# Value products of both heads in one product with a block-diagonal stationary operand

## The reference

```python
def _mhsa(x, Wq, Wk, Wv, Wr):
    B, n, D = x.shape
    dh = D // HEADS
    q = (x @ Wq).reshape(B, n, HEADS, dh)
    k = (x @ Wk).reshape(B, n, HEADS, dh)
    v = (x @ Wv).reshape(B, n, HEADS, dh)
    scores = jnp.einsum('bihd,bjhd->bhij', q, k)
    attn = jax.nn.softmax(scores, axis=-1)
    out = jnp.einsum('bhij,bjhd->bihd', attn, v).reshape(B, n, D)
    out = out + x @ Wr
    return jax.nn.relu(out)
...
embed_x = emb_table[X + offsets[None, :]]
att = embed_x
for i in range(LAYERS):
    att = _mhsa(att, WQ[i], WK[i], WV[i], WR[i])
att_output = jax.nn.relu(att.reshape(B, FLAT) @ Wlin)
h = embed_x.reshape(B, FLAT)
h = jax.nn.relu(h @ W1 + b1)
h = jax.nn.relu(h @ W2 + b2)
dnn_output = jax.nn.relu(h @ W3 + b3)
return jax.nn.sigmoid(att_output + dnn_output)
```

## Time and profile before

| What | Value |
|---|---|
| median of 3 runs | 2033.41 us (2029.62 to 2035.76) |
| profiled execution, its span | 2034.7 us |
| TensorE matmuls / weight loads busy | 94% / 83% of the span |
| VectorE / ScalarE / GpSimd busy | 83% / 66% / 44% |
| value products (L496), matmuls | 24576 |
| scores (L479), matmuls | 12288 |
| transposes (L464) | 3072 |

### The profile page before, as it was taken

The page is one execution under the profiler, slowest core; times in us unless marked ns, Lnnn a source line. Parts: engine busy times, 40 slices in busy tenths (PEclk is TensorE's granted clock), DMA queues, the critical chain, the costliest instruction groups (busy, mean ns, idle before and its releaser), DMA issues.

```text
span 2034.7 us, 105018 instructions
## 1 busy us (share of the span) xinstructions
PE 1914.9 (94%) x44960; PEld 1692.9 (83%) x44960; DVE 1690.5 (83%) x3771; ACT 1351.5 (66%) x3609; POOL 893.3 (44%) x949
## 2 busy tenths in 40 slices
PE   1499999999999999999999999999999999999998
PEld 0387888888888888888888888888888888888887
DVE  3477889889898888979888898888889898888987
ACT  1366666667666676766766776666776667676665
POOL 6544354444535454354544435354453545444000
PEclk9899999999999999999999999999999999999998
DMA  4210111111111111111111111111111111110000
GB/s 113 60 31 25 31 27 32 29 30 31 28 33 28 31 30 29 32 28 32 29 30 30 29 33 27 32 28 30 31 28 34 28 32 29 30 31 26 20 20 16
DMA packets 67859, 64.71 MB, mean 32 GB/s; under 512 B 24056, under 2 KB 54792, under 8 KB 67400
## 3 DMA queue, kind: packets, MB, share of 16 engines
q1 hardware_dynamic: 47432, 37.52, 6.3%
q0 software_dynamic: 19968, 20.49, 5.3%
HBM read 27.24 MB, written 0.01 MB: 13 GB/s over the span
## 4 chain that ended last, share of the span: by engine, by line
PE 86%; DVE 5%; issue 4%; ACT 3%; another core or an unknown queue 1%; POOL 1%; SPq 0%; DMA 0%; ACTq 0%
PE SV L479 20%; PE Ob L496 14%; PE X L464 12%; PE X L457 8%; PE X L459 5%; PE X L458 5%; PE Mb L432 3%; PE Mb L433 3%; PE Mb L434 3%; PE Ob L457 3%; PE Ob L458 2%; PE Ob L459 2%; PE Ob L423 2%; PE Mb L450 1%
## 5 line engine op out<-in xcount | busy, mean ns | idle before, releaser
L355 POOL DMA_INDIRECT emb<-L_rec_emb_table,idx_t x624 | 646.9, 1037 | 752.4 <-PE Ob L496 551.2
L742 DVE TENSOR_REDUCE den<-sd 103x16 f32<-103x624 f32 x384 | 308.0, 802 | 225.6 <-ACT sd L616 211.0
L479 PE MATMUL SV<-yv,xs 64*39 64x142 f32 x12288 | 456.0, 285 | 21.2 <-ACT v_sb L618 13.4
L479 PEld LDWEIGHTS SV<-yv,xs 64*39 64x39 f32 x12288 | 349.8, 113 | 68.0 <-issue 39.6
L600 ACT ACTIVATE xs<-Ob 128x312 f32<-128x312 f32 x256 | 110.4, 431 | 383.6 <-PE Ob L496 383.6
L722 DVE TENSOR_REDUCE mx<-SV 103x8 f32<-103x312 f32 x768 | 332.7, 473 | 37.0 <-PE SV L479 28.7
L496 PEld LDWEIGHTS Ob<-pt,v_sb 39*32 39x32 f32 x12288 | 272.1, 106 | 96.5 <-issue 96.0
L464 PE MATMUL X<-ident,pn 103*103 103x103 f32 x3072 | 343.0, 255 | 0.0
L496 PE MATMUL Ob<-pt,v_sb 39*32 39x39 f32 x12288 | 326.4, 198 | 8.9 <-issue 8.5
L332 POOL COPY xs<-embT 64x256 f32<-64x256 f32 x300 | 239.1, 797 | 211.6 <-ACT embT L560 80.7
L727 DVE TENSOR_TENSOR sd<-SV,mx 103x312 f32<-103x312 f32 x768 | 330.2, 470 | 0.1
(11 more groups left out here) (81 smaller groups left out, 2749.2 us busy)
## 6 DMA issues: line engine op xcount, KB each, us to landing
v_x<-v_sb SPq DMA_DIRECT2D x768, 39.0 KB
emb<-L_rec_emb_table,idx_t POOLq DMA_INDIRECT x624
xs<-L_rec_W SPq DMA_DIRECT2D x19, 256.0 KB
w<-L_rec_W SPq DMA_DIRECT2D x1, 512.0 KB
idx_in<-r_X SPq DMA_DIRECT2D x1, 312.0 KB, 3.8
b_b<-L_rec_b SPq DMA_DIRECT2D x1, 256.0 KB
b_b<-L_rec_b SPq DMA_DIRECT2D x1, 128.0 KB
w_b<-L_rec_W SPq DMA_DIRECT2D x1, 128.0 KB
```

The source lines that it names most:

```text
L355: nc.gpsimd.indirect_dma_start(out=emb[:, n % ER, f % 2 * D:(f % 2 + 1) * D], out_offset=None, in_=table, in_offset=bass.IndirectOffsetOnA ...
L479: last = nc.tensor.matmul(SV[64 * b:64 * b + F, at:at + YR], x_pair(u, e, p), yv[64 * e:64 * e + D, l, p, :], start=True, stop=True, skip_ ...
L742: nc.vector.tensor_reduce(den[:], pe_sb[:], AX.X, ALU.add).then_inc(den_ready, 1)
```

## The change

The 64-column padding of the probabilities goes: `pn` has 39 columns a head, so a transpose takes 78 columns and `pt` has 78 partitions, head 0 on 0 to 38 and head 1 on 39 to 77. The values of both heads go into one stationary operand `v_bd` of 78 rows and 64 columns: head 0's values in rows 0 to 38 and columns 0 to 31, head 1's in rows 39 to 77 and columns 32 to 63, zeros elsewhere, written once at the start. One product a sample gives both heads. All values reach `v_bd` by transfers, four a unit; `v_sb` and `v_bd` are laid out with the region innermost, so that each transfer writes 1024 bytes side by side in a partition, and the columns of a stationary operand stand eight elements apart. The copy to `v_sb` reads SV in that order. `VS` becomes 2; SyncE waits for the products of two units before, and ScalarE for the transfers of two units before.

```diff
--- before.py
+++ after.py
@@ -43,7 +43,7 @@
     G = UP
     SR = 256
     YR = HF + D
-    VS = 3
+    VS = 2
     PS = 2
     XS = 5
 
@@ -144,15 +144,15 @@
         x_lo = sb("x_lo", [128, XS, C], F32R)
         w_all = embT[:, 1].rearrange("q c b -> q (c b)")[:, 0:L * (3 * 128 + D)].rearrange("q (l c) -> q l c", l=L)
         yv = sb("yv", [128, L, UP, YR])
-        v_sb = sb("v_sb", [KR, VS, H, G, DH])
-        v_x = sb("v_x", [KR, VS, G, DH])
+        v_sb = sb("v_sb", [KR, VS, H, DH, G])
+        v_bd = sb("v_bd", [HF, VS, 2, D, G])
         mx = sb("mx", [KR, G, H])
         sd = sb("sd", [KR, G, H, F])
         pe_sb = sd
         den = sb("den", [KR, G, H])
         rd = sb("rd", [KR, G, H])
-        pn = sb("pn", [KR, PS, G, H, 64])
-        pt = sb("pt", [KR, G, 2, F])
+        pn = sb("pn", [KR, PS, G, H, F])
+        pt = sb("pt", [HF, G, 2, F])
         red = sb("red", [128, TILES * NP])
         w_in = red[0:D, 0:2 * L * D].rearrange("q (k d) -> q k d", d=D)
         wT = red[0:D, 2 * L * D:4 * L * D].rearrange("q (k d) -> q k d", d=D)
@@ -172,7 +172,7 @@
 
         sv_regions = SV[0:KR, :].rearrange("q (g w) -> q g w", w=SR)
         sv_scores = sv_regions[:, :, 0:HF].rearrange("q g (h f) -> q g h f", f=F)
-        sv_values = sv_regions[:, :, HF:HF + D].rearrange("q g (h c) -> q h g c", c=DH)
+        sv_values = sv_regions[:, :, HF:HF + D].rearrange("q g (h c) -> q h c g", c=DH)
 
         ld_w = sem("ld_w")
         ld_i = sem("ld_i")
@@ -315,9 +315,11 @@
 
             for u in range(TOTAL):
                 sp.wait_ge(v_ready, u + 1)
+                at_least(sp, o_ps, u - VS + 1)
                 for b in range(2):
-                    lo, hi = 64 * b, 64 * (1 - b)
-                    sp.dma_start(v_x[hi:hi + F, u % VS, :, :], v_sb[lo:lo + F, u % VS, 1 - b, :, :]).then_inc(v_moved[u % VS], 16)
+                    for h in range(H):
+                        sp.dma_start(v_bd[h * F:(h + 1) * F, u % VS, b, h * DH:(h + 1) * DH, :],
+                                     v_sb[64 * b:64 * b + F, u % VS, h, :, :]).then_inc(v_moved[u % VS], 16)
 
             sp.wait_ge(fin_act, 1)
             sp.dma_start(out.rearrange("(t p) o -> t (p o)", p=128), y_out[:]).then_inc(stored, 16)
@@ -339,7 +341,7 @@
             pool.wait_ge(pre_pool, 3)
             nc.gpsimd.affine_select(out=ident[:], in_=ident[:], compare_op=ALU.not_equal, fill=1.0, base=0,
                                     pattern=[[-1, 128]], channel_multiplier=1).then_inc(pre_pool, 1)
-            nc.gpsimd.memset(pn[:], 0.0).then_inc(pre_pool, 1)
+            nc.gpsimd.memset(v_bd[:], 0.0).then_inc(pre_pool, 1)
 
             def gather(t, f):
 
@@ -461,8 +463,8 @@
             def transposes(u, j):
 
                 for g in range(G // 2):
-                    last = nc.tensor.transpose(XB[j][0:KR, g * 128:g * 128 + KR],
-                                               pn[:, u % PS, j * (G // 2) + g, :, :].rearrange("q h f -> q (h f)")[:, 0:KR],
+                    last = nc.tensor.transpose(XB[j][0:HF, g * 128:g * 128 + KR],
+                                               pn[:, u % PS, j * (G // 2) + g, :, :].rearrange("q h f -> q (h f)"),
                                                ident[0:KR, 0:KR])
                 last.then_inc(t_ps, 1)
 
@@ -483,18 +485,15 @@
 
             def attended(u):
 
-                pe.wait_ge(v_moved[u % VS], 32 * (u // VS + 1))
+                pe.wait_ge(v_moved[u % VS], 64 * (u // VS + 1))
                 for p in range(UP):
                     j, pp, b = p // 4, p % 4 // 2, p % 2
                     if p % 4 == 0:
                         pe.wait_ge(pt_ready, 2 * u + j + 1)
                     for e in range(2):
                         g = (2 * j + e) * 2 + pp
-                        for h in range(H):
-                            lo, po = 64 * h, 64 * e + DH * h
-                            v = v_sb[lo:lo + F, u % VS, h, g, :] if b == h else v_x[lo:lo + F, u % VS, g, :]
-                            last = nc.tensor.matmul(Ob[po:po + DH, p * F:(p + 1) * F], v, pt[lo:lo + F, g, b, :],
-                                                    start=False, stop=True, skip_group_check=True)
+                        last = nc.tensor.matmul(Ob[64 * e:64 * e + D, p * F:(p + 1) * F], v_bd[:, u % VS, b, :, g],
+                                                pt[:, g, b, :], start=False, stop=True, skip_group_check=True)
                 last.then_inc(o_ps, 1)
 
             for k in range(NB):
@@ -614,7 +613,8 @@
                     at_least(act, pn_ready, u)
                     act.wait_ge(sd_ready, 2 * u + 2)
                     nc.scalar.activation(pe_sb[:], sd[:], ACTF.Exp).then_inc(e_ready, 1)
-                    at_least(act, o_ps, u - VS + 1)
+                    if u >= VS:
+                        act.wait_ge(v_moved[u % VS], 64 * (u // VS))
                     nc.scalar.copy(v_sb[:, u % VS, :, :, :], sv_values).then_inc(v_ready, 1)
                 if s < TOTAL and ts == H1T_AT:
                     act.wait_ge(h1T_ps, t + 1)
@@ -625,7 +625,7 @@
                     for j in range(2):
                         act.wait_ge(t_ps, 2 * u + j + 1)
                         nc.scalar.copy(pt[:, j * (G // 2):(j + 1) * (G // 2), :, :].rearrange("q g b f -> q (g b) f"),
-                                       XB[j][0:KR, :].rearrange("q (n f) -> q n f", f=64)[:, :, 0:F]).then_inc(pt_ready, 1)
+                                       XB[j][0:HF, :].rearrange("q (n f) -> q n f", f=64)[:, :, 0:F]).then_inc(pt_ready, 1)
                 if converted_at(s):
                     convert_high(*converted_at(s))
             act.wait_ge(fin_pe, 2)
@@ -744,7 +744,7 @@
                 nc.vector.reciprocal(rd[:], den[:]).then_inc(rd_ready, 1)
                 dve.wait_ge(rd_ready, s + 1)
                 at_least(dve, t_ps, 2 * (s - PS + 1))
-                nc.vector.tensor_tensor(pn[:, s % PS, :, :, 0:F], pe_sb[:], rd[:, :, :, None].to_broadcast([KR, G, H, F]),
+                nc.vector.tensor_tensor(pn[:, s % PS], pe_sb[:], rd[:, :, :, None].to_broadcast([KR, G, H, F]),
                                         ALU.mult).then_inc(pn_ready, 1)
                 if ts == H1T_AT - 2:
                     dve.wait_ge(l1_ps, t + 1)
```

## The result

The median of the changed kernel is 2470.16 us (2469.15 to 2470.98), against 2033.84 us of the kernel before, run beside it: a ratio of 1.214, with a 95% interval of 1.212 to 1.216. The forecast was 2113 us, the range 2012 to 2200. The direction was right and the size was not: 436 us were lost instead of 80. Rival (b), with a chance of 0.13 for three mechanisms together, had been priced at 2440 us, the price of its first one: a load at half rate.

What follows compares the result with a forecast made beforehand. TensorE was taken to bound the kernel, with ScalarE's copies meeting it at the scores. Value products add 88 us, fewer instructions save 8, all else nothing: 2033.4 + 80 = 2113 us, range 2012 to 2200.

Steps and rivals of the forecast that it cites:

- Rival (b): Value products: load at half rate, halves loading one behind the other, or load and matmul doing so; 2440 us, chance 0.13.
- the term of the value products: Value products on TensorE: rounds grow from 0.038 to 0.053 us, 0.23 us a step, 88 us over 384 steps.
- That the load is the bound: Value products: the 64-column load, 0.053 us a round, outlasts the matmul's 0.038 and sets the round.
- All 384 steps pay it: Whole step: longer value products delay TensorE's and ScalarE's roads to the scores equally, so each of 384 steps pays.
- Fewer instructions: TensorE: 64 fewer loads and matmuls a step take away a quarter of 30 us of holes: 8 us, bounds 0 and 30.
- Right at nothing: Transposes, probabilities' write and values' copy: each priced at no change, with upper bounds of 60 us for transposes, 0.6 us for the copy.
- rival (c): Values' copy: load bound as forecast, but the strided PSUM read slows the copy by 0.2 us; 2175 us, chance 0.15.
- The transfers stay hidden: Four transfers a step: data lands 4.2 us behind the values' copy, its reader comes 6.2 us behind; cost nothing.
- rival (d): Transfers: as forecast, but some arrive late, 0.3 us of wait in every fifth step; 2136 us, chance 0.07.
- rival (a): Value products: the wider load stays hidden behind 0.038 us and only holes shrink; 2025 us, down to 2003, chance 0.20.
- L541's 0.105 us: Closing product: a pair of 64-column loads takes 0.105 us at 1.2 GHz, halved to 0.053 us a round for 2.4 GHz.
- half-rate round of 0.106 us: Value products: a load at half rate makes a round 0.106 us, 1.07 us more a step, 411 us.

Runs made afterwards that it cites:

- N = 1: Changed kernel with the 64 columns of the stationary operand read side by side instead of eight elements apart (wrong values): 2115.06 us, 1.039 of the kernel before.
- The strided kernel before: Kernel before with only the value layout changed, region innermost, so its 32 columns stand eight elements apart: 2150.33 us, 1.057 of the kernel before.
- one head: Kernel before with the second head's value products left out, 32 a step instead of 64: 1942.98 us against 1987.57, 0.977.

## Why the prediction was wrong

**The failed step** is the term of the value products: "64 columns at 0.86 ns", taken from loads whose columns lie side by side, for an operand that has its columns 32 bytes apart. The round was put at 0.053 us and measured 0.121, 1.9 ns a column. The text saw that "no row of TensorE shows" this step, named the right rule, and still left its case out of the range with 0.13. Against rival (b) it cited L464 and L398. Both bear on its other halves (load and matmul one behind the other, the two halves one behind the other) and neither on the step, since their operands lie side by side. Three mechanisms were put into one rival under one price, and evidence against two of them was counted against the third. Its price for the half rate came near, 2440 against 2470, in part by luck: 1.07 us a step forecast, 1.24 measured from first to last; the products cost 482 us instead of 411, and 46 us came back.

**That the load is the bound** was right. With N = 1 the trace shows 0.90 us from first to last (0.80 to 0.85 forecast) and the time is 2115, 2 us from the forecast. But that nearness is luck: two errors cancel in it. The round is 0.058 us, not 0.053. The products take 0.303 us more a step in the mean (1.112 against 0.809), 116 us instead of 88, while 35 come back instead of 8:

| mean us | before | N = 1 | changed kernel |
|---|---|---|---|
| first value product to next projection | 0.809 | 1.112 | 2.064 |
| first projection into X (L457) to the first into Ob | 1.659 | 1.625 | 1.610 |
| first transpose to first score | 0.873 | 0.813 | 0.823 |
| first score to first value product | 1.114 | 1.113 | 1.107 |

**"All 384 steps pay it" by as much** was too strong. TensorE now starts the scores 0.05 to 0.06 us sooner behind the transposes, and the projections into Ob 0.03 to 0.05 us sooner behind those into X. In the kernel before, the scores started right behind the end of the values' copy (0.143 to 0.146 us) in 173 of 361 steps; with N = 1 in 60, in the changed kernel in 75. ScalarE's road is the later one in far fewer steps. The strided kernel before (2150 us) shows that this is not all the count of instructions: it keeps its 64 products, they take 0.385 us more, 148 us, and it loses 116.

**Fewer instructions** were sized from the wait on "issue" at the products alone, 110.7 us, of which 81 were set apart as the change of array shape. That split was right: 0.21 us stays in each step. But the savings lie also where no wait is named: in the mean time of the products (0.763 against a median of 0.724 before, 0.697 for both with one head: the holes within the products are gone, and the round is 0.036 instead of 0.038) and at the scores. Bounds of 0 to 30 were too narrow; 36 to 45 were measured.

The holes differ between the chips more than between the kernels. In the first trace of the kernel before, 23 of 361 steps take over 0.3 us more than the median from products to projection, 23 us in all; most stand 24 steps apart, one a tile. With N = 1, on the same chip, there are still 22 such steps and 18 us, and only the kernels with rounds of 0.12 us have none. On the second chip the kernel before has 13 (7 us), and those with fewer instructions none.

**Right at nothing:** the transposes (0.87 us for eight, 0.89 in the earlier trace rows), the probabilities' write, and the values' copy, so rival (c) falls: 593 ns with PSUM read 1 KB apart. That rule of the Trainium skill (Advanced Engine Details and Errata, PSUM Cachelines), that every two elements read one after the other should lie side by side, doesn't show in this copy. The transfers stay hidden, so rival (d) falls: the last packet of four lands a median 4.1 us behind the copy (4.2 forecast) and 3.3 us ahead of its reader, 1.6 at the least. That the new loads would overlap the matmuls was right too, so rival (a) fails on the load's length and not on the row groups.

**Not the clock.** The strided load's rate doesn't follow it. The two stretches are windows on the products of one step and of the last one (busy time and count of each engine, granted clock, DMA), and below them the last products in the timeline:

```profile
1004.60:1006.70 2.10, 2.10 (x36) 2.02 (x32) 2.10 (x7) 0.00 (x0) 0.00 (x0) 1.00 0.23 63
2457.00:2459.00 2.00, 2.00 (x32) 1.94 (x32) 0.00 (x0) 1.70 (x2) 0.00 (x0) 0.50 0.00 0
```

```profile
2456.93 2.15 PE L495 MATMUL Ob<-pt,v_bd 78*64 78x39 f32 x32
```

With 2.4 GHz granted (1.00) the 32 products take 2.13 us, with 1.2 GHz (0.50) 2.15, and the round is 0.121 us at either. A load side by side does follow the clock. The last step of the kernel with right values and side-by-side columns, window and timeline, runs at 1.2 GHz too:

```profile
2048.78:2050.50 1.72, 1.72 (x33) 1.72 (x32) 0.00 (x0) 1.63 (x2) 0.00 (x0) 0.50 0.00 0
```

```profile
2048.78 1.94 PE L497 MATMUL Ob<-pt,v_bd 78*64 78x39 f32 x32
```

From first to last these products take 1.63 us, where a step at 2.4 GHz takes 0.90: a round of 0.107 us against 0.058, 1.67 ns a column against 0.91. That is the size of the other error. L541's 0.105 us is right for 1.2 GHz, and halving it gave 0.053 where 0.058 was measured. It also bounds the price of the step: 0.121 against 0.058 us at 2.4 GHz, but 0.121 against 0.107 at 1.2. The forecast's half-rate round of 0.106 us is not what was measured either; the strided load costs 0.121.

**Open.** Why the scores wait less for the transposes' side when the products have fewer instructions or take longer was not settled; the table shows that they do. Of the 6 us (of 45 and of 38) that the two intervals don't hold, 4 to 5 lie in the first 21 steps and 2 to 3 between the first score and the first value product. Why the kernel before is 2.2% faster on the second chip is not known either. Of those 46 us, 32 lie in the start-up: the 22nd unit's value products start 218.6 us into the span on the first chip and 186.6 on the second, and in that stretch the granted clock is at 1.2 GHz for 24 us on the first and never on the second. The rest lies in the products of the later steps (a mean of 0.763 us against 0.809, at medians of 0.724 and 0.727), most of it in the holes between them. The granted clock over the whole run reads 0.998 against 0.991.

## What to carry to other kernels

Lay the columns of a stationary operand side by side, at most 8 bytes apart for fp32. At 16 and at 32 bytes its load took 1.9 ns a column at 2.4 GHz instead of 0.91, and about as much in the smaller shape tried (39 rows, 32 columns). The copy that writes the values is the cheaper place to reorder them: it took 592 to 593 ns in every order tried. Merging two small products into one with zeros saves instructions and no loading time: the load's columns (0.91 ns each) stand against the round that the moved columns allow, and where the load is the longer, it sets the round. When several mechanisms are put into one rival, give each its own evidence and chance before they are added up.

## What the runs showed of the hardware beside this

- With the columns side by side, the load's time goes by their number and not by the rows: a round of 0.058 us for 64 columns on 39 rows and on 78. It follows the clock: 0.107 us at 1.2 GHz.
- A strided load has its own rate, 1.9 ns a column, with 32 or 64 columns; the 64-column one keeps it at either level of the clock (rounds of 0.121 us at both).
- Leaving the scores' array shape (64 x 64 places) for another costs about 0.12 us a step; products that keep it start 0.99 us instead of 1.11 behind the first score (one kernel).
- Kernels with 32 value products a step instead of 64 (as many loads fewer), at a round of 0.036 to 0.038 us, were 36 to 45 us faster over 384 steps, some 0.1 us a step.
